# Statistics instructions for the normalisations, and another order of the expert and context products, in a two-layer decoder on one core

## The chip, the cores and the metric

The kernel runs on one core of one Trainium2 chip, as one program. The metric is the device time of one execution in microseconds (us). The kernel before took 1017.04 us as the median of three runs (1016.49 to 1020.86).

## The reference

Input `x` has 4 sequences of 256 tokens with 128 channels, the context 4 x 512 tokens. Six blocks are added to `x` one after the other, each on a layer norm of `x`:

```python
x = x + L0_attn(layernorm(x))          # causal, 16 heads of 8, weights plus low-rank weights
x = x + L0_xattn(ctx, layernorm(x))    # 16 heads of 64; keys: normed context and latents; normed latents ask
x = x + L0_ffn(layernorm(x))           # attention, then 8 routed experts and one shared expert
x = x + L1_attn(layernorm(x))          # causal attention with clipped scores
x = x + L1_xattn(layernorm(x), ctx, ctx, mask)   # one head of 128
x = x + L1_ffn(layernorm(x))           # base product and low-rank experts
# layernorm(x) = (x - mean(x)) / sqrt(var(x) + 1e-5), over the 128 channels
```

`L0_xattn` and `L0_ffn` norm their input, itself a layer norm, once more: `layernorm(layernorm(x))`. `L0_ffn` norms a third time, after its attention and ahead of its experts.

## The kernel before, in words

`x` lies in SBUF as 8 tiles of 128 tokens x 128 channels (`x[P, 8, 128]`). Each engine has its own program, written out by hand in the order in which it runs; semaphores tie them. An engine works strictly in that order, so a wait holds all that is behind it. The stages follow each other: attention `att0`, cross attention, `att1`, experts, `att2`, `single` (the one-head cross attention) and `mixture`. The long loops are inside the attentions (16 groups of four heads) and the cross attention (8 head pairs x 4 sequences x 2). What the change touches are the seams between them.

**Normalisations.** A table `jobs` lists 22 of them, each on four tiles (128 x 512 numbers): `n0` to `n5` (the norm of `x` ahead of each block), `ctx` 0 to 3, and the second norms `lat`, `ln1` (of `z`, written by `again`) and `ln2` (of `xin`). Each job is a chain through three engines. On VectorE `centre` (L1294) adds up each token (L1298) and subtracts the mean (L1299); ScalarE squares the result (`square_jobs`, L1010); VectorE's `variances` adds up the squares (L1306); GpSimd's `rstd_jobs` (L1852) makes the power -1/2 in two instructions (L1857, L1858); VectorE's `scale` multiplies (L1312) and lets the consumer go through `normed`. TensorE then transposes the four tiles (`transposes`, L468), ScalarE copies them out, and products follow (L518 to L521).

**Cross operands.** Between `att0` and the cross attention TensorE multiplies query and key weights (L494) into four banks, ScalarE copies them to `A_all` (L1089), and eight groups of transposes of the context pass through two banks (L508), each copied out by ScalarE (L1100, L1013). ScalarE's program has squares of `n1` ahead of `A_all`, those of `lat` 0 in the middle, those of `lat` 1 ahead of the second four groups. VectorE's `cross_latents` (L1494) comes last before the first query product.

**Shared expert and routing.** SyncE issues the load of the eight experts' first weights (`w1all`) once the cross attention has left its memory, and the shared expert's weights (`w1b`, `w2b`, L435 to L437) when the first half of `xin` is written, into the arena. ScalarE and VectorE split `w1b` into a high and a low part. TensorE runs `shared_up` (three products for each of 8 tiles of hidden numbers), the gate, `shared_down` (64 products), and between these the products that rank and find tokens (`ranks_of`, `tokens_of`). VectorE works the routing out in some 40 small linked instructions; GpSimd then gathers the tokens of 15 sorted tiles by indirect DMA (L1929), and results are scattered back (L1940), fetched (`back`, L447) and added to `x` (L1701).

**Context keys and values.** `single` first makes the keys (`wk4`, four products, L878) and values (`wv4`, 16 products, L883) of the context, which hang on nothing but `ctxT`, written during the cross operands. They lie in the arena, ahead of the queries of the normed `x`.

## Time and profile before

| | us |
|---|---|
| median of the runs | 1017.04 (1016.49 to 1020.86) |
| the profiled execution | 1019.7 |
| its span in the trace | 1017.9 |
| TensorE matmuls busy | 915.8 |
| VectorE busy | 680.0 |
| ScalarE busy | 547.6 |
| GpSimd busy | 205.5 |

The profiled execution lies 2.7 us above the median; its span leaves out 1.8 us of start and end. Busy times are sums over the whole span and say little of the seams. Times in the rows below are us from the start of the span unless marked ns. In a row of the timeline, a bracket gives how long the engine had been idle before the instruction and what released it.

### The profile page before, as it was taken

How to read it: one execution, taken by the hardware profiler on the slowest of the kernel's cores; microseconds unless marked ns; L12 is line 12 of the kernel's file. 1: busy time of each engine (PE TensorE's matmuls, PEld its weight loads, DVE VectorE, ACT ScalarE, POOL GpSimd, SP SyncE). 2: the span in 40 equal slices, each digit the busy share in tenths (PEclk: the TensorE clock that was granted, in tenths of full speed). 3: DMA queues.
4: the chain of work that ended last, by engine and by line, in shares of the span. 5: the costliest groups of instructions: out<-in, count | busy, mean ns of one | idle time of the engine just before them, and what ended most of it. 6: DMA issues, size and time to landing. Idle time of an engine off the chain costs nothing. (4 is left out here: it accounts for less than half of the span.)

```text
span 1017.9 us, 21416 instructions
## 1 busy us (share of the span) xinstructions
PE 915.8 (90%) x6712; PEld 742.9 (73%) x6712; DVE 680.0 (67%) x1706; ACT 547.6 (54%) x1515; POOL 205.5 (20%) x321
## 2 busy tenths in 40 slices
PE   5899968999999999999999699997876788888888
PEld 3677758888888888888888487776766555555665
DVE  5878766666665666666653578885523799999574
ACT  2667655555555555555553267774444466666351
POOL 2544220000000000000000233330153344443100
PEclk9999999999999999999999799999888899999996
DMA  7000000000000000000000200002121000000000
GB/s 267 2 0 0 0 1 1 2 1 1 0 0 0 0 0 0 0 0 0 0 0 1 82 2 0 0 0 81 55 41 51 0 2 0 0 0 0 21 1 21
DMA packets 9398, 16.14 MB, mean 16 GB/s; under 512 B 816, under 2 KB 5040, under 8 KB 8976
## 3 DMA queue, kind: packets, MB, share of 16 engines
q1 hardware_dynamic: 8400, 13.68, 3.9%
q0 software_dynamic: 960, 1.97, 0.9%
q8 instruction: 22, 0.36, 0.1%
q14 instruction: 16, 0.13, 0.0%
HBM read 13.61 MB, written 2.03 MB: 15 GB/s over the span
## 5 line engine op out<-in xcount | busy, mean ns | idle before, releaser
L1514 DVE TENSOR_REDUCE xnegmax<-psum 128x1 f32<-128x768 f32 x128 | 122.3, 955 | 139.8 <-PE psum L649 139.6
L1156 ACT ACTIVATE arena<-psum,xnegmax 128x768 f32<-128x768 f32 x128 | 115.4, 902 | 139.5 <-DVE xnegmax L1514 97.8
L536 PE MATMUL psum<-arena 128*128 (+2 forms) x768 | 187.3, 359 | 1.8 <-POOL arena L1872 0.5
L1872 POOL TENSOR_TENSOR arena<-arena,pack_a 128x256 f32 (+1 forms) x192 | 122.5, 646 | 146.3 <-PE psum L540 71.0
L1051 ACT ACTIVATE arena<-psum,arena 128x256 f32<-128x256 f32 (+1 forms) x256 | 112.1, 445 | 57.7 <-PE psum L555 28.4
L555 PE MATMUL psum<-pack_a,arena 128*128 128x128 f32 x704 | 110.9, 278 | 30.2 <-ACT arena L1058 24.2
L536 PEld LDWEIGHTS psum<-arena 128*128 128x128 f32 x768 | 122.0, 192 | 11.7 <-issue 4.6
L555 PEld LDWEIGHTS psum<-pack_a,arena 128*128 128x128 f32 x704 | 79.8, 142 | 58.6 <-issue 24.3
L667 PE MATMUL psum<-pack_a,arena 128*128 128x128 f32 x768 | 106.8, 275 | 0.2 <-ACT arena L1147 0.2
L647 PE MATMUL psum<-kv_high,xq_high 128*128 128x384 f32 x256 | 101.0, 394 | 3.3 <-DVE xq_low L1503 1.7
L1147 ACT ACTIVATE arena<-psum 128x512 f32<-128x512 f32 x128 | 75.9, 593 | 42.5 <-PE psum L667 42.5
L667 PEld LDWEIGHTS psum<-pack_a,arena 128*128 128x128 f32 x768 | 87.4, 141 | 13.9 <-issue 12.3
L679 PE MATMUL psum<-arena,xv 128*64 128x256 f32 x768 | 89.9, 383 | 0.0
L648 PE MATMUL psum<-kv_low,xq_high 128*128 128x384 f32 x256 | 86.4, 338 | 0.0
L649 PE MATMUL psum<-kv_high,xq_low 128*128 128x384 f32 x256 | 86.4, 337 | 0.0
L1907 POOL COPY acur<-A_all 128x128 f32 (+1 forms) x18 | 5.7, 318 | 387.4 <-PE psum L632 387.4
L1398 DVE COPY arena<-psum 128x384 f32<-128x384 f32 (+1 forms) x96 | 58.9, 616 | 27.0 <-PE psum L555 27.0
L679 PEld LDWEIGHTS psum<-arena,xv 128*64 128x64 f32 x768 | 52.3, 137 | 31.0 <-issue 6.0
L1391 DVE SCALAR_TENSOR_TENSOR arena<-arena,ones_ 128x256 f32<-128x256 f32 x128 | 73.2, 574 | 0.1
L1058 ACT ACTIVATE arena<-psum 128x512 f32<-128x512 f32 (+1 forms) x96 | 55.3, 577 | 3.7 <-PE psum L555 3.6
L540 PE MATMUL psum<-causalb,identb 128*128 128x128 bf16 x256 | 56.3, 220 | 0.0
L639 PEld LDWEIGHTS psum<-pack_v,kvT 128*128 128x128 f32 x396 | 53.9, 191 | 2.7 <-DVE xv L1519 0.9
(282 smaller groups left out, 1670.9 us busy)
## 6 DMA issues: line engine op xcount, KB each, us to landing
w1all<-in_w SPq DMA_DIRECT2D x1, 2048.0 KB, 9.3
arena<-in_w SPq DMA_DIRECT2D x1, 2048.0 KB, 9.4
pack_v<-in_pack_v SPq DMA_DIRECT2D x1, 1088.0 KB, 9.6
pack_l<-in_pack_l SPq DMA_DIRECT2D x1, 1079.5 KB, 12.6
pack_q<-in_pack_q SPq DMA_DIRECT2D x1, 1024.0 KB, 7.4
pack_f<-in_pack_f SPq DMA_DIRECT2D x1, 684.0 KB, 10.7
pack_a<-in_pack_a SPq DMA_DIRECT2D x1, 649.0 KB, 6.4
pack_b<-in_pack_b SPq DMA_DIRECT2D x1, 578.0 KB, 9.5
```

Source lines behind the costliest of these rows:

```text
L536: last = mm(bank[j][:, u * T:u * T + keys], qm[:, j, u * P:(u + 1) * P], kT[:, bass.ds(b * T, keys)], start=True, stop=not a.causal)
L555: last = transpose(bank[4 + j % 2][:, i * P:(i + 1) * P], prob[:, j, u, k * P:(k + 1) * P], ident)
L647: mm(out, xq_high[:, u % 2, tile], kv_high[:, u // 2, keys], start=True, stop=False)
L648: mm(out, xq_high[:, u % 2, tile], kv_low[:, u // 2, keys], start=False, stop=False)
L649: last = mm(out, xq_low[:, u % 2, tile], kv_high[:, u // 2, keys], start=False, stop=True)
L667: last = transpose(bank[4 + (3 * u + c) % 2][:, (2 * i + h) * P:(2 * i + h + 1) * P], xprob[:, u % 2, h * KEYS + kt * P:h * KEYS + (kt + 1 ...
L679: mm(bank[6][XD * a:XD * (a + 1), 0:T], xv[:, b, kt * P + XD * a:kt * P + XD * (a + 1)], xpT[:, b % 2, a, kt * T:(kt + 1) * T], start=(kt ...
L1051: last = activation(prob[:, j, u, 0:keys], bank[j][:, u * T:u * T + keys], ACT.Exp, bias=negmax[:, j, u:u + 1], accum_out=sums[:, it, u * ...
L1147: activation(xpT[:, (mu // 2) % 2, mu % 2, 2 * c * T:2 * (c + 1) * T], bank[4 + (3 * mu + c) % 2][:, :], ACT.Copy).then_inc(sx["pT_act"], 1)
L1156: activation(xprob[:, u % 2, half * KEYS:(half + 1) * KEYS].rearrange("p (c w) -> p c w", c=2), src, ACT.Exp, bias=xnegmax[:, u % 2, half: ...
L1514: v.tensor_reduce(xnegmax[:, u % 2, half:half + 1], banks_pair(half), AX.XY, ALU.max, negate=True)\
L1872: pool.tensor_tensor(qm[:, j, :], qT[:, bass.ds(b * T, T)], headmask[:, bass.ds(g * HG + j, 1)].broadcast_to([P, T]), ALU.mult)\
```

## The change

- **Normalisations.** `centre`, `variances` and the squares on ScalarE are gone, with the memory `centred` and `squares`. `measure` runs four `bn_stats` on 128 x 128 and, after a wait for them, four `bn_aggr`, which write mean and variance. `scale` is four `tensor_scalar` on 128 x 128 (subtract the mean, multiply). The second norms `lat` and `ln1` are not measured: GpSimd works out their factor from the first norm's variance in four instructions. In most places `scale` of the first half now stands behind `measure` of the second.
- **Shared expert.** Its weights get a place of their own (`shared_w`), and their loads are issued right behind `w1all`, without the wait for `xin`. `weight_low` stands ahead of `scale` of the first half. `w1now` moves out of `hid`. `ranks_of` comes ahead of `shared_down`; of `shared_down(1)` one tile comes before `tokens_of`, three after.
- **Context keys and values.** They move from the front of `single` to `context_operands`, behind the experts and ahead of `att2`, in the memory of `w1all`.
- **`mixture`.** TensorE waits for `x_parts` 7 ahead of the gate's bank.

```diff
+        shared_w = sb("shared_w", [P, 2 * B * KEYS - 2 * NT * P - 4 * F])
+        w1b, w2b, iota = shared_w[:, 0:F], shared_w[:, F:F + FT * D], shared_w[:, F + FT * D:F + FT * D + P]
...
-            sp.wait_ge(sf["xin_ready"], 1)
-            sp.dma_start(w1b[:, 0, :], w1_d[E]).then_inc(sf["shared_in"], 16)
+            sp.dma_start(w1b, w1_d[E]).then_inc(sf["shared_in"], 16)
...
                 shared_up(1)
-                shared_down(0, range(0, 2))
                 ranks_of()
-                shared_down(0, range(2, 4))
-                shared_down(1)
+                shared_down(0)
+                shared_down(1, range(0, 1))
                 tokens_of()
+                shared_down(1, range(1, 4))
...
+            def context_operands():
+                pe.wait_ge(sf["gelu_done"], 2 * FT + FT * SORTED)
                 for c in range(4):
+                    if c == 2:
+                        pe.wait_ge(sf["expert_ready"], SORTED)
                     for t in range(4):
                         last = mm(bank[(6, 7, 2, 3)[c]][:, t * P:(t + 1) * P], ctxT[:, (4 * c + t) * P:(4 * c + t + 1) * P],
                                   col("l", "wv4"), start=True, stop=True)
                     last.then_inc(sg["proj_psum"], 1)
+                for c in range(4):
+                    mm(bank[(4, 5, 0, 1)[c]][:, :], col("l", "wk4"), ctxT[:, c * BANK:(c + 1) * BANK], start=True, stop=True)\
+                        .then_inc(sg["proj_psum"], 1)
+                pe.wait_ge(sg["proj_act"], 4)
+                pe.wait_ge(sg["proj_dve"], 4)
...
+            context_operands()
             attention(att2, z, "n3", col("l", "w3"), col("l", "wp3"))
...
+            def measure(keys):
                 for key in keys:
                     k, src, _, (after, value) = jobs[key]
                     dve.wait_ge(after, value)
+                    for t in range(4):
+                        chain.did(v.bn_stats(moments[:, k % 4, t, :], src[:, t, :]))
+                    chain.wait(dve)
+                    for t in range(4):
+                        last = v.bn_aggr(moments_of(key)[:, t, :], moments[:, k % 4, t, :])
+                    last.then_inc(var_ready, 1)
 
             def scale(keys):
...
+                    for t in range(4):
+                        rstd = stat[:, k % 4, 3, t:t + 1]
+                        if key in parents:
+                            last = v.tensor_scalar(dst[:, t, :], src[:, t, :], rstd, None, ALU.mult)
+                        else:
+                            last = v.tensor_scalar(dst[:, t, :], src[:, t, :], moments_of(key)[:, t, 0:1], rstd,
+                                                   ALU.subtract, ALU.mult)
+                    last.then_inc(normed, 1)
...
                 for h in range(2):
...
-                    centre([("ln2", h)])
+                    measure([("ln2", h)])
                     if h:
                         z_low_half(0)
-                    variances([("ln2", h)])
-                    if h == 0:
+                    else:
                         weight_low()
                     scale([("ln2", h)])
...
-                    normalise([("n3", c)])
+                    measure([("n3", c)])
+                scale([("n3", 0), ("n3", 1)])
...
+            measure([("n1", 0)])
             add_to_x(att0.out_psum, 1, 1)
...
+            measure([("n1", 1)])
+            scale([("n1", 0), ("n1", 1), ("lat", 0), ("lat", 1)])
...
+            measure([("n2", 0)])
             add_to_x(sx["out_psum"], 1, 1)
...
+            measure([("n2", 1)])
+            scale([("n2", 0), ("ln1", 0), ("n2", 1)])
...
+                    if key in parents:
+                        parent = jobs[parents[key]][0]
+                        first = stat[:, parent % 4, 3, :]
+                        pool.wait_ge(rstd_ready, parent + 1)
+                        link(pool.tensor_tensor(work, first, first, ALU.mult))
+                        link(pool.tensor_tensor(work, work, moments_of(parents[key])[:, :, 1], ALU.mult))
+                        link(pool.tensor_scalar(work, work, EPS, None, ALU.add))
```

## Rows read from the trace of the kernel before

**Rows 1.** The page, part 1: busy us, share of the span, instructions, by engine.
```profile
PE 915.8 (90%) x6712; PEld 742.9 (73%) x6712; DVE 680.0 (67%) x1706; ACT 547.6 (54%) x1515; POOL 205.5 (20%) x321
```
**Rows 2.** Windows: stretch, length; busy us by engine, PEclk, DMA share, GB/s.
```profile
162.00:570.00 408.00, 405.85 (x2969) 351.08 (x2967) 239.63 (x419) 214.39 (x476) 5.89 (x18) 1.00 0.02 5
...
778.00:790.00 12.00, 1.20 (x9) 0.97 (x8) 3.78 (x9) 1.06 (x3) 2.32 (x4) 0.72 0.20 61
...
802.00:947.00 145.00, 119.29 (x938) 84.61 (x938) 139.28 (x572) 95.92 (x269) 62.27 (x93) 0.99 0.00 0
```
**Rows 3.** Groups: busy, mean ns, idle before and releaser; last, timeline of one scaling.
```profile
L1306 DVE TENSOR_REDUCE stat<-squares 128x4 f32<-128x512 f32 x22 | 14.9, 682 | 7.8 <-ACT squares L1010 7.6
...
L1312 DVE TENSOR_TENSOR z<-centred,stat 128x512 f32<-128x512 f32 x18 | 12.8, 715 | 14.5 <-POOL stat L1858 14.3
...
L1299 DVE SCALAR_TENSOR_TENSOR centred<-stat,x 128x512 f32<-128x512 f32 x12 | 8.3, 692 | 0.4
L1298 DVE TENSOR_REDUCE stat<-x 128x4 f32<-128x512 f32 x12 | 8.2, 684 | 2.9 <-DMA x<-in_x 2.5 <-DVEq L1750 0.2
...
141.20 0.69 DVE L1312 TENSOR_TENSOR z<-centred,stat 128x512 f32<-128x512 f32 x1 [1.41 <-POOL stat L1858]
```
**Rows 4.** VectorE's small instructions: timeline (start, us), and one group.
```profile
24.98 0.29 DVE L1366 TENSOR_REDUCE arena<-psum 128x1 f32<-128x128 f32 x1
...
25.18 0.41 DVE L1369 TENSOR_REDUCE arena<-psum 128x1 f32<-128x256 f32 x1
...
731.18 0.17 DVE L1658 TENSOR_SCALAR chosen<-psum 128x15 uint32<-128x15 f32 x1 [1.38 <-PE psum L808]
731.27 0.16 DVE L1659 SCALAR_TENSOR_TENSOR arena<-psum,pack_f 128x15 f32<-128x15 f32 x1
...
785.41 1.14 DVE L1701 SCALAR_TENSOR_TENSOR x<-arena,x 128x128 f32<-128x128 f32 x4 [5.36 <-DMA arena<-expert_rows]
...
L1673 DVE COPY arena<-w1all 128x512 f32 x15 | 6.4, 427 | 7.7 <-issue 7.7
```
**Rows 5.** Timeline, first groups of att0.
```profile
34.83 0.52 PE L555 MATMUL psum<-pack_a,arena 128*128 128x128 f32 x3 [4.29 <-DVE arena L1398]
```
**Rows 6.** Timeline, cross operands.
```profile
134.31 2.06 PE L494 MATMUL psum<-pack_q 64*128 64x128 f32 x32
...
137.72 1.06 ACT L1089 ACTIVATE A_all<-psum 128x512 f32<-128x512 f32 x2
...
141.65 1.97 PE L508 MATMUL psum<-pack_a,ctx_x 128*128 128x128 f32 x8 [4.26 <-ACT ctxT L1100]
...
148.39 0.81 DVE L1494 TENSOR_SCALAR kvT<-psum,pack_b 128x512 f32<-128x512 f32 x1 [0.75 <-PE psum L468]
```
**Rows 7.** Timeline, from the cross attention to att1.
```profile
572.78 1.09 PE L468 MATMUL psum<-pack_a,z 128*128 128x128 f32 x4 [3.56 <-DVE z L1312]
...
581.12 0.66 PE L468 MATMUL psum<-pack_a,z 128*128 128x128 f32 x4 [1.67 <-DVE z L1312]
```
**Rows 8.** Timeline, from att1 to the first gathered tile.
```profile
706.18 0.66 PE L468 MATMUL psum<-pack_a,z 128*128 128x128 f32 x4 [2.54 <-DVE z L1312]
...
709.19 0.77 PE L778 MATMUL psum<-z_high,w_high 128*128 128x512 f32 x1 [2.35 <-DVE z_low L1582]
...
732.25 1.21 POOL L1929 DMA_INDIRECT arena<-rows,chosen  x1 [21.23 <-DVE chosen L1661]
```
**Rows 9.** The context's products: values as a group, keys in the timeline.
```profile
L883 PE MATMUL psum<-pack_l,ctxT 128*128 128x128 f32 x32 | 4.1, 275 | 0.0
...
958.22 3.60 PE L878 MATMUL psum<-ctxT,pack_l 128*128 128x512 f32 x8
```
**Rows 10.** Timeline, from the experts to att2.
```profile
791.72 1.09 PE L468 MATMUL psum<-pack_a,z 128*128 128x128 f32 x4 [11.99 <-DVE z L1312]
...
800.41 0.75 DVE L1352 TENSOR_SCALAR arena<-psum,pack_l 128x512 f32<-128x512 f32 x1
```
**Rows 11.** Timeline, first scores of single.
```profile
967.02 1.02 PE L896 MATMUL psum<-arena 128*128 128x512 f32 x2
```

More of the change, by code:

```diff
@@ L407, in decoder, with measured, moments_of @@
                     job(("ln2", h), quarter(xin, h), quarter(z2, h), (sf["xin_ready"], h + 1))
+        def measured(key):
+            return sum(1 for other in jobs if other not in parents and jobs[other][0] <= jobs[key][0])
+        def moments_of(key):
+            return stat[:, jobs[key][0] % 4, 0:2, :].rearrange("p a (t s) -> p (a t) s", s=2)
         FIRST_JOBS = [("n0", 0), ("n0", 1)]
@@ L956, in mixture @@
                 pe.wait_ge(sl["zT_act"], 1)
+                pe.wait_ge(x_parts, NT - 1)
                 gate(0)
@@ L1292, in link @@
                 chain.wait(dve)
-            def centre(keys):
+            def measure(keys):
                 for key in keys:
@@ L1696, in experts @@
                     v.tensor_copy(expert_rows[:, i, :], bank[2 + i % 2][:, 0:D]).then_inc(sf["expert_ready"], 1)
+                dve.wait_ge(sf["w1_split"], 1 + SORTED)
+                dve.wait_ge(loaded["l"], 16)
+                for c in range(4):
+                    dve.wait_ge(sg["proj_psum"], c + 1)
+                    v.tensor_tensor(quarter(vx, c), tiles(bank[(6, 7, 2, 3)[c]][:, :]),
+                                    col("l", "bv4").unsqueeze(1).broadcast_to([P, 4, D]), ALU.add)\
+                        .then_inc(sg["proj_dve"], 1)
                 dve.wait_ge(sf["mixed"], 2 + NT)
```

168 lines of the change are left out of this document (47 added, 121 removed).

## The prediction

> **What bounds the kernel now.** I read the page first, then the table of windows by stage, then the groups of instructions, and then the timeline of each seam between two stages. The page gives TensorE 90% of the span [rows 1], but that is a mean over unlike stages. The windows part them: the cross attention keeps TensorE busy for 405.85 of 408 us, the loop of `att2` keeps VectorE busy for 139.28 of 145 us, and behind the experts, from 778 to 790, TensorE has 1.20 us of work in 12 [rows 2]. The diff touches no loop of an attention. What it can win or lose lies in the seams, so I take each seam by itself: what releases TensorE there, and when would that come after the change? VectorE's total busy time matters nowhere.
>
> **Prices.** One measured norm before: sum 0.69, centre 0.69, a wait for ScalarE's square of about 0.75 and the sum of squares 0.69 [rows 3], so some 2.8 us until GpSimd may begin; GpSimd's two steps hold VectorE for 1.41, and the scaling takes 0.69 [rows 3]. After: four `bn_stats`, a wait, four `bn_aggr`. The trace has neither, so I bound them by neighbours. Reductions of 128 columns start 0.20 apart and last 0.29, tiny instructions start 0.09 apart and last 0.17 [rows 4]. Low end: 3 x 0.20 + 0.29 + 0.03, then 3 x 0.09 + 0.17, is 1.36. High end, every instruction at its whole duration: 4 x 0.29 + 4 x 0.17 + 0.03, 1.87. Cheaper than the low end is excluded, since no instruction of either width starts closer; dearer than the high end is not (rivals 3 and 4). I take 1.45, close to the low end, since the four of a row are independent as L1366 and L1369 are. The norm is ready for GpSimd 1.35 us sooner, and VectorE is spared some 0.6 us of work (three instructions of 512 columns against eight small ones). The scaling becomes four instructions of 128 columns: four with one column operand took 1.14 us, 0.26 apart [rows 4]. I take 1.04 for it, 0.35 dearer than now, with 0.8 (0.20 apart) and 1.4 (whole durations of 0.35) as ends. A copy of 512 columns from SBUF to SBUF took 0.427 us [rows 4], faster than the 0.715 of the scaling with two tensors, which speaks for the cheap end.
>
> The Trainium skill ("VectorE: DVE Perf Modes", TRN2 errata) says that each instruction that reads SBUF pays a fixed latency, so that many small tiles pay it many times: a rule that speaks against this change. By its (N+151)/0.96 formula, an estimate, one of 128 columns costs 0.29 us, which is the duration of L1366, while starts 0.20 apart show that much of it overlaps; by that page a measurement would cost at least 1.9 instead of 1.45, the third rival.
>
> **The seams, one by one, in us won.**
> - *Start and first groups of `att0`.* The scaling of `n0` is on the path: -0.35. Between the first two groups VectorE holds TensorE for 4.29 us [rows 5] with context norms. Two centrings and two sums of squares (3.9) become two measurements (2.7), +1.2, and two scalings -0.7. Together +0.2; with the ends of the prices -1.5 to +1.2.
> - *Cross operands.* The first two banks of weight products are full about halfway through L494, at 135.3, but ScalarE copies them out only at 137.72, because squares stand ahead: +2.4. Two more squares in the chain of copies: +1.1. TensorE therefore idles about 1 us instead of 4.26 ahead of the third group of transposes, and eight of them don't take 1.97 [rows 6] but about 1.1 (four took 0.66 at full clock [rows 8]): +0.9. Sum 4.4, some more where waits close up: 4.7. What is late next is the second norm of the latents: two measurements, GpSimd's chain of four steps for each `lat` (two take 1.41 with their waits [rows 3]; four, by an estimate from that, 1.9), the scaling; I get 142.5 for it, and transposes of the context last until 142.3, so both meet. `cross_latents` then starts at 143.6, not 148.39 [rows 6]. 3.7 to 5.3.
> - *Into `att1`.* TensorE has nothing from 569.22 on (572.78 less 3.56 [rows 7]), when the second half of `x` can be added. Now `scale` of `n2` 0 and `ln1` 0 stand behind `measure` of `n2` 1: 0.6 + 1.45 + 1.04 + 0.85 gives 573.2, so the first transposes come 0.4 later. The second half isn't measured any more: its transposes wait 1.67 us today [rows 7]; they would follow the first half's products at once: +1.7. Net +1.3.
> - *`ln2` and the shared weights.* Today the loads start when `xin` is written, and the split of the weights holds `scale`; transposes come 2.54 us after TensorE ran out at 703.64 [rows 8]. Loaded long before, the weights cost VectorE 0.6 inside GpSimd's time. Measured 701.7, factor 703.0, scaled 704.1: +2.0, and `shared_up` moves with it, at 707.1 instead of 709.19. The loads' own issue on SyncE lies behind `w1all`, under the end of the cross attention, and nothing waits there.
> - *Routing.* 16 of the 64 passes of `shared_down` no longer stand ahead of the ranks; they come when VectorE has picked, so about 1.5 sooner. Then 40 passes, then `tokens_of`; the gathers start 2.0 sooner than 732.25 [rows 8] counted from the same start. Three tiles of `shared_down` are now behind them and put the first sorted tile's transpose 0.4 later, but the second is no longer waited for, and the gap there closes. I take +2.0 at the end of the loop; 0 to 3.5.
> - *Context products.* Values 4.1, keys about 3.5 (3.60 with the pass record's tail) [rows 9]: 7.6 us of TensorE in a hole of 11.99 us [rows 10] that ends when `n3` is scaled. They begin at 779.7 and end at 787.4; VectorE's four additions and ScalarE's four copies trail by 0.7, while VectorE would wait for the fetched rows until 785.41 [rows 4]. Cost nothing, with 3.5 us of cover; without cover each us counts.
> - *Into `att2`.* The first half is scaled behind the second's measurement: 785.41 + 1.14 + 1.45 + 1.14 + 1.35 + 1.04 is 791.5, as today. The second half is ready 4.5 us sooner, but TensorE is busy with the first at half clock anyhow. VectorE's memsets come off the path, and query copies no longer begin at 800.41 [rows 10]; the last of those that the scores need ends at 801.0, not 802.4: +1.4.
> - *`single`.* The products ended in scores at 967.02 [rows 11], 8.8 us after they began at 958.22 [rows 9]. After: add 0.7, measure 1.45, scale `n4` 0 1.04 (now behind the second measurement, not under the projection), transposes 0.6, copy 0.65, queries 0.9, VectorE's copy 0.75: 964.5 at full clock, +2.5. TensorE would stand idle 3.2 us first. After 2.54 us it came back at full clock (0.66 for four transposes [rows 8]), after 3.56 at half (1.09 [rows 7]). Half clock would cost two transposes 0.45 each and two passes each of queries and scores 0.86, all but 0.3 of the gain. I take the middle: +1.3.
> - *`mixture`.* `n5` a bit sooner, but TensorE is bound by its base products there: +0.2. The wait for `x_parts` is satisfied by the time of the transposes: 0.
>
> **Sum.** 0.2 + 4.7 + 1.3 + 2.0 + 2.0 + 1.4 + 1.3 + 0.2 = 13.1. The profiled execution of 1019.7 would become 1006.6; the median of the runs lies 2.7 lower, so 1004.
>
> **Rivals.**
> 1. *TensorE stays at full clock in the seams.* Idle times become shorter at three of them. One half's projections are four passes of 512 columns (0.43 each, from the keys) and eight of 128 (0.13) [rows 9], 2.7 us more at half clock. For it: att1's second half, `shared_up`, whose gaps get shorter. Against: the gap ahead of `ln1` 0 grows. Three such places and 1.2 in `single`: 9 us more, 995.
> 2. *The expert loop gives it back.* From the first gather [rows 8] to the hole behind it [rows 2] it takes 46 us for 15 tiles, where GpSimd's gathers and scatters and waits that the trace doesn't explain share the pace. If its end doesn't move, 4.0 are lost: 1008. For it: GpSimd's descriptors are the same; against: they start sooner.
> 3. *The small instructions don't overlap.* Nine measurements at 1.87 (+0.42) and ten scalings at 1.4 (+0.36) on the path cost 7.4: 1011.5. Against: two starts 0.20 apart and two 0.09 apart [rows 4]. The errata rule of "VectorE: DVE Perf Modes" in the Trainium skill speaks for it.
> 4. *Slower.* `bn_stats` or `bn_aggr` is a longer instruction than any that I bound it by. About 115 small ones lie on the path (nine times eight, ten or eleven times four), so the gain is gone at 0.11 us above my price for each; at 0.2 above, 23 us are added and 13.1 won: 1027. Nothing in the trace speaks for it but that neither instruction is in it.
> 5. *The context products don't fit under the wait*, because a bank or the last copy holds them past 791.5: +1 to +4, 1007.
>
> **How the numbers follow.** Forecast 0.50, with its own range of 999 to 1009; rival 1 0.17; rival 2 0.17; rival 3 0.10; rival 4 0.04; rival 5 0.02. The range runs from 992, between rival 1 and the forecast, to 1012, rival 3. A measurement of this kernel can tell about 0.5%, 5 us, from no change. Faster by more than that (under 1012): all but rival 4 and half of rival 3 and a little of the rest, 0.92; within 0.5%: 0.05; slower: 0.03.
>
> **What would show it.** `bn_stats` about 0.20 apart and `bn_aggr` about 0.1; ScalarE's copies to `A_all` right behind the first weight products, and the first cross query some 5 us sooner after `att0`; transposes of `ln2` 0 about 0.5 us behind the projection; 7.6 us of context products inside the hole behind the experts with the clock full, and the hole otherwise as long; scores of `single` 6 us behind its projection. Wrong it would be if TensorE waited longer ahead of the first halves (their scaling is behind a second measurement everywhere), or if the expert loop ended no sooner.

## The result and the profile after

The changed kernel takes 1004.86 us (median of 4 runs, 1003.74 to 1009.54), the kernel before 1017.27 beside it: a ratio of 0.9875 with a 95% interval of 0.9851 to 0.9900, 12.4 us less. A second set of six runs, beside the experiments, gave 1006.95 against 1019.34, 0.9894 (0.9864 to 0.9924). The profiled execution took 1005.44 us, its span is 1003.6 where that of before was 1017.9: 14.3 less, of a forecast of 13.1.

The page's busy times, to be read beside [rows 1], and two windows that answer to [rows 2]: the hole behind the experts (now 767 to 779) and the loop of `att2`.

```profile
PE 916.4 (91%) x6712; PEld 743.2 (74%) x6712; DVE 668.1 (67%) x1850; ACT 534.3 (53%) x1493; POOL 207.7 (21%) x329
...
767.00:779.00 12.00, 7.79 (x47) 5.52 (x46) 8.43 (x33) 2.75 (x4) 3.66 (x6) 0.92 0.19 55
...
790.00:935.00 145.00, 119.53 (x955) 85.36 (x954) 138.97 (x572) 97.61 (x272) 60.75 (x90) 1.00 0.00 0
```

VectorE does 144 instructions more in 11.9 us less, ScalarE has lost 13.3 us of squares, TensorE does the same. In the hole TensorE now works for 7.79 us of 12. The prices of the new instructions, from the groups (busy us, mean ns of one, idle before), to be held against [rows 3]; then one measurement in the timeline:

```profile
L1286 DVE BATCH_NORM_STATS2 moments<-x 128x6 f32<-128x128 f32 x48 | 10.4, 279 | 3.0 <-DMA x<-in_x 2.5 <-DVEq L1733 0.2
...
L1289 DVE BATCH_NORM_AGGREGATE stat<-moments 128x2 f32<-128x6 f32 x72 | 6.8, 157 | 0.6
...
L1303 DVE TENSOR_SCALAR z<-x,stat 128x128 f32<-128x128 f32 x48 | 13.1, 338 | 2.9 <-POOL stat L1834 2.9
L1301 DVE TENSOR_SCALAR z<-z,stat 128x128 f32<-128x128 f32 x16 | 4.7, 353 | 2.1 <-POOL stat L1834 2.0
...
946.08 0.87 DVE L1286 BATCH_NORM_STATS2 moments<-x 128x6 f32<-128x128 f32 x4
946.99 0.38 DVE L1289 BATCH_NORM_AGGREGATE stat<-moments 128x2 f32<-128x6 f32 x4
947.29 1.08 DVE L1303 TENSOR_SCALAR z<-x,stat 128x128 f32<-128x128 f32 x4
```

A measurement takes 1.29 us (946.08 to 947.37) and frees VectorE after 1.21; four scalings take 1.08. The forecast had 1.45 and 1.04.

The seams in the timeline, in the order of [rows 5 to 8], then [rows 10] and [rows 11]:

```profile
33.90 0.87 PE L567 MATMUL psum<-pack_a,arena 128*128 128x128 f32 x3 [3.00 <-DVE arena L1384]
...
135.63 2.06 ACT L1085 ACTIVATE A_all<-psum 128x512 f32<-128x512 f32 x4 [5.47 <-PE psum L506]
...
138.51 1.14 PE L520 MATMUL psum<-pack_a,ctx_x 128*128 128x128 f32 x8 [1.00 <-ACT ctxT L1094]
...
143.75 0.81 DVE L1480 TENSOR_SCALAR kvT<-psum,pack_b 128x512 f32<-128x512 f32 x1 [0.83 <-PE psum L480]
...
568.71 1.01 PE L480 MATMUL psum<-pack_a,z 128*128 128x128 f32 x4 [4.18 <-DVE z L1301]
...
575.79 0.60 PE L480 MATMUL psum<-pack_a,z 128*128 128x128 f32 x4
...
696.64 0.66 PE L480 MATMUL psum<-pack_a,z 128*128 128x128 f32 x4 [1.01 <-DVE z L1303]
...
720.37 1.24 POOL L1904 DMA_INDIRECT arena<-rows,chosen  x1 [19.97 <-DVE chosen L1646]
...
779.44 1.09 PE L480 MATMUL psum<-pack_a,z 128*128 128x128 f32 x4 [4.65 <-DVE z L1303]
...
789.33 0.75 DVE L1338 TENSOR_SCALAR arena<-psum,pack_l 128x512 f32<-128x512 f32 x1 [1.90 <-PE psum L530]
...
948.42 1.11 PE L480 MATMUL psum<-pack_a,z 128*128 128x128 f32 x4 [3.10 <-DVE z L1303]
...
953.14 1.79 PE L914 MATMUL psum<-kvx,arena 128*128 128x512 f32 x2
```

In the brackets stands how long TensorE waited. Ahead of the third group of context transposes it fell from 4.26 us to 1.00, ahead of `ln2` from 2.54 to 1.01, and ahead of the second half of `ln1` from 1.67 to nothing. Ahead of the first halves it grew at two places: 4.18 at `ln1` (3.56 before), and 3.10 at `n4`, where before the change the context's products filled the time. At `n3` it is 4.65 where it was 11.99, but the products of the context (767.62 to 774.79) now fill the rest of that hole. The same instants in both traces, with what the forecast's terms add up to by then:

| begins (us) | before | after | moved | forecast |
|---|---|---|---|---|
| second projection of `att0` | 130.54 | 130.67 | +0.1 | -0.2 |
| first query product, cross attention | 149.30 | 144.66 | -4.6 | -4.9 |
| first scores of `att1` | 587.93 | 579.98 | -8.0 | -6.2 |
| first transposes of `ln2` | 706.18 | 696.64 | -9.5 | -8.2 |
| first gather | 732.25 | 720.37 | -11.9 | -10.2 |
| last expert row copied | 779.76 | 767.82 | -11.9 | -10.2 |
| first scores of `att2` | 802.52 | 790.87 | -11.7 | -11.6 |
| first scores of `single` | 967.02 | 953.14 | -13.9 | -12.9 |
| last addition to `x` | 1014.44 | 1000.18 | -14.3 | -13.1 |

### The profile page after: what moved, and what is told of

It reads as the page before. It is cut to its first block, busy times and chain, and to the rows that moved or that the text cites. A ratio compares the mean times of both kernels' runs of the same rounds, so it can differ in the third digit from the quotient of the medians.

```text
span 1003.6 us, 21535 instructions
## 1 busy us (share of the span) xinstructions
PE 916.4 (91%) x6712; PEld 743.2 (74%) x6712; DVE 668.1 (67%) x1850; ACT 534.3 (53%) x1493; POOL 207.7 (21%) x329
## 4 chain that ended last, share of the span: by engine, by line
PE 75%; DVE 13%; issue 5%; ACT 4%; DMA 1%; DVEq 1%; another core or an unknown queue 0%; ACTq 0%; POOL 0%; SPq 0%
PE psum L548 10%; PE psum L679 9%; PE psum L691 9%; PE psum L567 5%; PE psum L659 5%; PE psum L660 4%; PE psum L661 4%; PE psum L651 4%; DVE arena L1377 4%; PE psum L644 3%; PE psum L585 3%; PE psum L619 2%; DVE arena L1355 2%; PE psum L760 1%; PE psum L591 1%
## 5 line engine op out<-in xcount | busy, mean ns | idle before, releaser
L679 PEld LDWEIGHTS psum<-pack_a,arena 128*128 128x128 f32 x768 | 87.4, 141 | 13.9 <-issue 12.3
```

The lines of the kernel that those rows point to most:

```text
L679: last = transpose(bank[4 + (3 * u + c) % 2][:, (2 * i + h) * P:(2 * i + h + 1) * P], xprob[:, u % 2, h * KEYS + kt * P:h * KEYS + (kt + 1 ...
```

## The experiments

Ratios are to the kernel before, run beside each group; an interval is 0.0020 to 0.0038 to either side. Since the program's beginning and end differ from one profile to the next (below), stretches inside the traces are compared, not instants.

### What each part is worth

The third part undone (`e1_context_back`; abridged. On VectorE the scaling of the first half of `n4` also goes back under the projection, as before the change, so the two are measured together):

```diff
-            context_operands()
             attention(att2, z, "n3", ...)
 def single():
+    for c in range(4): mm(bank[2 + c], wk4, ctxT[c]) ...
+    values(0); values(1); transposes n4 0; values(2); queries(0); values(3); transposes n4 1
```

> The changed kernel with the third part alone undone: keys and values of the context are multiplied inside single again, in the old order (keys, two values, transposes, the rest), and nothing stands in the hole behind the experts. The recorded theory: behind the experts they cost nothing, and in single they were mostly beside the normalisation already, so that the move is worth about 1.3 us there: this kernel takes 0.8 to 1.8 us more than the changed one, all of it between the last projection of att2 and the first scores of single. A rival: the products and the four additions on VectorE delay n3 (the changed kernel's transposes of n3 come 5.9 us after the rows are fetched, 779.44 less 773.49, against 6.3 before, 791.72 less 785.41); then the first transposes of n3 come sooner after the fetched rows here than 5.9 us, and the kernel is within 0.5 us of the changed one. A second rival: 7.2 us of TensorE work (3.74 and 3.60) stood on the path of single, and 4 us or more come back.

1006.19 us, 0.9885 (0.9860 to 0.9910), beside 0.9875 and 0.9894 for the changed kernel: level with it. The transposes of `n3` come 5.95 us behind the fetched rows (774.73 to 780.68), as in the changed kernel (5.95), so the products delay nothing there. The first scores of `single` come 8.6 us behind the last projection of `att2` (945.36 to 953.99), 7.8 in the changed kernel: the move wins 0.8 us there, the low end of what the theory gave (1.3 in e2 and e6 below, whose `single` is that of the changed kernel, at a granted clock of 0.68 over the four us from 948, where it was 0.50 in the changed kernel's profile), and the 7.2 us of products were nearly all hidden in the old place too. That is too little to be seen in times that scatter by 6.

The second part undone (`e2_shared_back`), its order alone undone (`e6_order_back`), and the changed kernel itself beside the latter (`e0_changed`):

```diff
+            sp.wait_ge(sf["xin_ready"], 1)          # e2 only
             sp.dma_start(w1b, w1_d[E])...
+                shared_down(0, range(0, 2))         # e2 and e6
                 ranks_of()
-                shared_down(0)
-                shared_down(1, range(0, 1))
+                shared_down(0, range(2, 4))
+                shared_down(1)
                 tokens_of()
-                shared_down(1, range(1, 4))
```

> The changed kernel with the second part undone: the loads of the shared expert's weights wait for xin again, and two tiles of shared_down stand ahead of the ranks again, all others behind them and ahead of tokens_of. The recorded theory: the weights' loads cost 1.5 to 2.0 us ahead of the first transposes of ln2 (in the changed kernel these follow the projection after 1.01 us; here again after some 2.5), and the order of the products 2.0 to 2.5 us, seen at the first gather and again at the end of the loop over the sorted tiles: 3.5 to 4.5 us more than the changed kernel. The rival that the loop over the sorted tiles gives it back, paced by the gathers and scatters and by stalls that do not move: the first gather comes 3.5 to 4.5 us later but the last expert row only 1.5 to 2.0 later, and so does the kernel.

> The changed kernel with the old order of the products alone: two tiles of shared_down ahead of the ranks, the others behind them and ahead of tokens_of; the weights are loaded as in the changed kernel. The recorded forecast gives the order 2.0 us at the end of the loop: 2 us more than the changed kernel beside it. Theory A: the first gather comes 0.7 to 2 us later against the end of the picks, but the loop from the first gather to the last expert row takes 47.5 instead of 50: equal to the changed kernel or up to 1.5 us less. The transposes of ln2 come about 1 us behind the projection as in the changed kernel, not 2.7 as with the loads undone.

> The changed kernel itself once more, beside the three below on the same chip: its median there, and a second profile of the same program. Two stretches are looked at. The loop over the sorted tiles, from the first gather to the last expert row, took 47.45 us in its profile (720.37 to 767.82), but 50.14, 49.91 and 50.67 in the three experiments that have the same order of shared_down, and 47.51 and 47.65 in the two kernels with the old order (the kernel before, and the changed kernel with the second part undone). Theory A: the new order brings the gathers 2 us forward and the loop gives it back, so that 47.45 was an exception: here 49 to 51. Theory B: the loop varies by 3 us in any order; then nothing is foretold. The other stretch is mixture, from the last addition in single to the last addition to x: 24.29 us there, 23.1 to 29.0 in the others. Theory: the same instructions, at TensorE's half clock for a shorter or longer part; 22.5 to 29 here, the more the longer the granted clock is at half.

e2: 1004.30 us, 0.9855 (0.9835 to 0.9876). e6: 1004.20, 0.9856 (0.9832 to 0.9880). e0: 1006.95, 0.9894 (0.9864 to 0.9924). e2 was expected 3.5 to 4.5 us slower than the changed kernel, and is not slower. The new order of the products wins nothing; by the medians of e6 and e0 it costs 2.7 us, but their intervals overlap, and at the last expert row the traces differ by 1.1 us (620.9 and 622.0 behind the first cross scores). The traces say why nothing is won. Start of the first gather, the restart of the loop and the first expert row, in e0 (new order) and in e6 (old order):

```profile
717.72 1.24 POOL L1904 DMA_INDIRECT arena<-rows,chosen  x1 [19.93 <-DVE chosen L1646]
...
724.04 2.08 PE L838 MATMUL psum<-arena 128*128 128x128 f32 x8 [0.39 <-issue]
...
726.13 1.91 PE L838 MATMUL psum<-arena 128*128 128x128 f32 x8
...
729.35 0.43 DVE L1658 COPY arena<-w1all 128x512 f32 x1 [2.96 <-PE psum L838]
729.36 1.14 ACT L1193 ACTIVATE arena<-psum,pack_f 128x128 f32<-128x128 f32 x4 [5.01 <-PE psum L838]
...
730.64 0.58 PE L848 MATMUL psum<-arena 128*128 x1 [2.60 <-ACT arena L1193]
...
732.75 0.29 DVE L1681 COPY arena<-psum 128x128 f32<-128x128 f32 x1 [2.97 <-PE psum L848]
```

```profile
720.26 1.24 POOL L1904 DMA_INDIRECT arena<-rows,chosen  x1 [22.20 <-DVE chosen L1646]
...
727.26 1.14 ACT L1193 ACTIVATE arena<-psum,pack_f 128x128 f32<-128x128 f32 x4 [1.35 <-issue]
...
730.41 1.06 PE L838 MATMUL psum<-arena 128*128 128x128 f32 x8
...
731.88 0.29 DVE L1681 COPY arena<-psum 128x128 f32<-128x128 f32 x1 [4.21 <-PE psum L848]
731.89 1.14 ACT L1193 ACTIVATE arena<-psum,pack_f 128x128 f32<-128x128 f32 x4 [3.14 <-PE psum L838]
```

In e0 the first tile's products begin at 724.04 and take 2.08 us by the record (a matmul's end is modelled), but ScalarE's gelu of them begins only at 729.36, 3.2 us behind that end; in e6 it begins 0.14 us behind it. VectorE and ScalarE stand still and go on together, 11.64 us behind the first gather. The brackets say for what: both wait for TensorE's signal that these products are done. TensorE itself does not stand with them: its records show the second tile's products from 726.13 to 728.04, then it waits 2.60 us for ScalarE's gelu and goes on at 730.64. The expectation of e9 below counts it among the engines that go on together, which is not what these rows show. In e6 VectorE and ScalarE go on 11.62 us behind the first gather, again at signals of TensorE (which by its records still works at 730.41), but there the first gelu (727.26) and the first tile's second product came ahead of the standstill. The gather is 2.3 us earlier in e0 counted from the first cross scores, the first tile is not, and the standstill catches it one stage less far. So the loop, from the first gather to the last expert row, takes:

| order | profiles | us |
|---|---|---|
| old | before, e2, e6, e5, e11 | 47.5, 47.7, 47.7, 47.7, 47.6 |
| new | after; e0, e1, e3, e4, e7, e8, e10 | 47.4; 51.1, 50.1, 49.9, 50.7, 51.0, 51.0, 50.1 |

The profile of the changed kernel was the exception (there they went on at +10.12 us); seven others of the same order took 2.5 to 3.7 longer, e3 among them, where they went on at +10.91.

The loads' place was worth 2.3 us where the forecast put it (the first product of the shared expert is 550.3 us behind the first cross scores in e6 and 552.5 in e2), and nothing at the gather (573.2 us behind them in e6, 573.0 in e2): with early weights and the old order the picks are ready at 710.43 and the ranks' product starts at 712.23, behind two tiles of `shared_down`; with late weights it starts 0.25 behind the picks. Late weights with the new order were not run.

The normalisations alone (`e5_norms_alone`: both diffs above on the changed kernel):

> The changed kernel with the second and the third part undone together: the normalisations by statistics instructions alone (with the squares gone from ScalarE). The recorded forecast sums the parts so: 13.1 in all, of which the order in the routing 2.0, the shared weights some 1.0 to 2.0, the products of the context and what hangs on them about 1: the normalisations alone some 8 to 9, 4 to 5 us more than the changed kernel. What the experiments say so far: the context products back cost nothing measurable, the order back won about 2.7 us, the loads back cost 1.7 at their place, so this one is level with the changed kernel or up to 2 us faster: 1004 to 1007, and nearly all of the gain of 13 us is that of the normalisations.

1010.16 us, 0.9911 (0.9888 to 0.9934): 8.6 us less than before by the medians, the 8 to 9 of the forecast's sum rather than my expectation. Its profile is of a run of 1002.82, and the six other runs took 1008.75 to 1011.40, so what makes most of its runs slower than e2's (1003.37 to 1006.27), which differs by the context products' place alone, is in no trace here; all that is on record of them is the granted clock over the whole run, 0.961 to 0.967 in those six and 0.967 to 0.970 in e2's. With the new order there was no such difference (e1 against e0). Whether the move behind the experts is worth 0 or some 5 us stays open.

### What paces the loop over the sorted tiles

Four gathers ahead (`e9_four_gathers`), twelve ahead (`e10_twelve_gathers`):

```diff
-AHEAD = NT        # 8
+AHEAD = 4         # e9; 12 in e10
```

> The changed kernel with four gathers issued ahead instead of eight; the others follow behind the scatters, one each, as before. In eight of the ten profiles so far TensorE, VectorE and ScalarE stand still in the loop over the sorted tiles and go on together 11.61 to 11.68 us after the first gather began, when the eight gathers (1.25 us apart, the last ends 10.0 us after the first began) and their transfers are done; with the new order of shared_down this stands ahead of the first tile's gelu, with the old order behind it, and the loop from the first gather to the last expert row takes 50.0 to 51.1 instead of 47.5 to 47.7. Theory: the standstill belongs to the row of gathers and ends when its transfers are done. With four it ends some 6.6 us after the first gather, before the first gelu is due (8.4 us), so the first expert row comes some 3 us sooner (12 us behind the first gather, not 15), the loop takes 46 to 48 us and the kernel 2 to 4 us less than the changed kernel, if GpSimd, which now alternates scatter and gather (2.57 us a pair) for eleven tiles instead of seven, does not set the pace. Rival: the standstill has to do with the code of the loop (its first pass through it) and not with the gathers: it stays at the same place, and the kernel is not faster.

> The changed kernel with twelve gathers issued ahead instead of eight. Theory (the standstill belongs to the row of gathers): the engines go on together some 16.6 us after the first gather began, not 11.65, or stand still twice; the first expert row comes 18 to 20 us behind the first gather, not 15; behind it the loop is faster, since GpSimd has only three gathers left among the scatters. Rival (it belongs to the code of the loop): they go on at 11.65 as before and the loop is the same or shorter.

e9: 1018.57 us (twelve runs, 1016.21 to 1026.40, the profiled one 1025.74), 1.0004 (0.9980 to 1.0028), as slow as before the change. e10: 1005.67 over six runs, of which one took 1811.43 us, for a cause that no trace shows; the other five took 1002.05 to 1012.22, median 1004.52, ratio 0.9865 (0.9827 to 0.9902), level with the changed kernel. First e9, then e10:

```profile
719.05 1.24 POOL L1904 DMA_INDIRECT arena<-rows,chosen  x1 [19.95 <-DVE chosen L1646]
...
731.09 0.29 DVE L1681 COPY arena<-psum 128x128 f32<-128x128 f32 x1 [3.11 <-PE psum L848]
...
734.77 1.00 POOL L1915 DMA_INDIRECT expert_rows<-arena,chosen  x1 [0.30 <-issue]
736.07 0.97 POOL L1904 DMA_INDIRECT arena<-rows,chosen  x1 [0.30 <-issue]
737.02 0.33 PE L830 MATMUL psum<-pack_a,arena 128*128 128x128 f32 x1 [3.99 <-DMA arena<-rows,chosen]
```

```profile
718.72 1.24 POOL L1904 DMA_INDIRECT arena<-rows,chosen  x1 [19.94 <-DVE chosen L1646]
...
736.09 0.29 DVE L1681 COPY arena<-psum 128x128 f32<-128x128 f32 x1 [6.71 <-remote]
736.09 1.14 ACT L1193 ACTIVATE arena<-psum,pack_f 128x128 f32<-128x128 f32 x4 [5.37 <-remote]
```

Both halves of the theory hold for the standstill: with four gathers the common restart at +11.6 is gone and the first expert row comes at +12.04 as expected; with twelve VectorE and ScalarE go on at +17.37 (16.6 expected), after a shorter halt of both that ends at +10.23, and the first row is copied at +17.37. It goes with the number of gathers in a row, not with the code. That the shorter row makes the kernel faster was wrong: behind it TensorE waits for each gather (3.99 us at 737.02), which now follows a scatter, and the loop takes 63.7 us. With twelve it takes 50.1, of which the part behind the first row takes 32.7, where it took 36.1 in e0. In e10's brackets stands "remote", a releaser that the profile could not name; by the program VectorE waits there for TensorE's second product and ScalarE for its first one, as in e6. Why TensorE's signals come so late while gathers are issued the traces don't say.

### The first half scaled ahead, and TensorE's clock

`e3_first_ahead`:

```diff
             measure([("n2", 0)])
+            scale([("n2", 0), ("ln1", 0)])
             add_to_x(sx["out_psum"], 1, 1)
             measure([("n2", 1)])
-            scale([("n2", 0), ("ln1", 0), ("n2", 1)])
+            scale([("n2", 1)])
```

and so for `n3` and `n4`, where the copy of the first queries and the first scores also come ahead of the second scaling and the second transposes.

> The changed kernel, but with the first half scaled before the second half is measured: in front of att1 (n2 and ln1 of the first half scaled before the second half is added to x), in front of att2 (n3) and in single (n4, where the copy of the first queries is ahead of the second scaling too, and the first scores ahead of the second transposes). Theory: the forecast's step that named the scaling behind a second measurement was right on the place and too small on the price, because VectorE waits 5.6 us for the second half of the projection (564.57) when it could scale: TensorE's wait of 4.18 us ahead of ln1 goes nearly to zero, the wait ahead of n3 loses 1.1, and the scores of single come 3 to 4.5 us sooner, TensorE's clock with them. 7 to 10 us less than the changed kernel, some 996. Rival: the second half, whose measurement and scaling nothing brings forward, is what is late next; the gain is then 2 us at att1, 0 at att2 and 2 in single: 3 to 5 us, some 1001.

1003.77 us (999.45 to 1004.55), 0.9836 (0.9813 to 0.9858), against 0.9875 and 0.9894 for the changed kernel: 4.0 and 5.9 us less by the ratios (1.1 and 3.2 by the medians), near the rival's 3 to 5 and far from the theory's 7 to 10. The first of the two pairs of intervals overlaps a little. Ahead of `att1`:

```profile
561.73 0.60 PE L480 MATMUL psum<-pack_a,z 128*128 128x128 f32 x4
...
567.63 2.00 DVE L1300 TENSOR_SCALAR z<-z,stat 128x128 f32<-128x128 f32 x4
567.79 2.33 POOL L1849 TENSOR_TENSOR arena<-arena,pack_a 128x256 f32<-128x256 f32 x4 [0.33 <-DVE arena L1337]
...
569.68 1.11 PE L480 MATMUL psum<-pack_a,z 128*128 128x128 f32 x4 [3.55 <-DVE z L1300]
```

TensorE's wait ahead of the first half is gone (4.18 us in the changed kernel), and 3.55 of it stand ahead of the second, with half clock behind it. From the first cross scores to the first scores of `att1` it is 429.8 us against 430.7. Ahead of `att2`, from the fetched rows to the first scores, 15.95 against 17.38 and 16.90 (changed kernel, e0), but e1, e2, e5 and e6, without this edit, have 16.0 to 16.2: only the first transposes are surely sooner, 5.42 behind the fetched rows instead of 5.95. In `single` it works in full: the first scores come 3.3 us behind the first transposes of `n4` instead of 4.7, and those 0.7 behind the projection instead of 3.1.

Eight products that nothing reads ahead of `n3` (`e4_filled`):

```diff
+                pe.wait_ge(sg["proj_dve"], 2)
+                for _ in range(8):
+                    mm(bank[7][:, :], col("l", "wk4"), ctxT[:, 0:BANK], start=True, stop=True)
```

> The changed kernel with eight more products of 512 columns (128x512, 0.43 us each at full clock, 3.4 us) on TensorE behind the context products, into a bank whose contents are done with; nothing reads them. They fill most of the 4.65 us in which TensorE stands still ahead of the transposes of n3 and release nobody. Theory: the half clock there (four transposes 1.09, two key and query products 2.07 and 1.91, eight value products 1.92 us) comes from the standstill: filled, they take 0.6, 1.1, 1.0 and 1.05, and the first scores of att2 come 2.5 to 3.3 us sooner, the kernel 2 to 3.3 us less. Rival: the clock falls behind the experts for another reason (the load of the loop before), and the products change nothing or delay the transposes by up to 0.5: 0 to 0.5 us more.

1007.90 us (1002.18 to 1011.82), 0.9886 (0.9855 to 0.9918).

```profile
775.84 7.03 PE L902 MATMUL psum<-ctxT,pack_l 128*128 128x512 f32 x16
...
782.71 0.60 PE L480 MATMUL psum<-pack_a,z 128*128 128x128 f32 x4
```

I had sized them wrongly: 0.43 us is one of the two passes of such a product, so eight take 7.03 and put the transposes 2 us late. But the clock is the theory's: four transposes in 0.60, at full clock, where they took 1.09 behind a standstill of 4.65 us, and the first scores follow them by 8.0 us, where the nine profiles with the old wait have 10.0 to 11.5. As the transposes are 2 us late, the kernel is no faster.

Products at the end (`e7_end_filled`), and the first half ahead with three products at `n3` and those at the end (`e8_ahead_filled`):

```diff
+                    if n >= NT - 1:                 # single's loop, behind the weighted sums
+                        mm(bank[6][:, :], col("l", "wk4"), ctxT[:, 0:BANK], start=True, stop=True)
                 transposes("n5", z, 0, sl["zT_psum"])
+                mm(bank[7][:, 0:T], col("l", "wk4"), ctxT[:, 0:T], start=True, stop=True)
```

(the last line behind the second transposes of `n5` too)

> The changed kernel with products that nothing reads in TensorE's standstills near the end: one of 512 columns (0.88 us) in each of the last three steps of single's loop, and one of 256 columns (0.44 us) behind each of the two groups of transposes of n5, where TensorE waits 0.7 to 0.8 us for the copy. Theory: the granted clock falls to half some 5 to 8 us after the sparse stretch at the end of single and stays there for 8 to 25 us, by chance; without the sparse stretch it stays at full, and mixture, from the last addition in single to the last addition to x, takes 22 to 23 us in place of 23 to 29: median 1.5 to 3 us less than the changed kernel beside it, and the spread of the runs smaller. Rival: the fall comes for another reason (the many small products, or the ones with 6 columns and with one row), mixture is no shorter, and the products add up to 0.5 us.

> The first half scaled ahead of the second half's measurement everywhere (as in the third experiment), three products of 512 columns that nothing reads behind the context products (2.64 us, so that they end before n3 is scaled; the eight of the fourth experiment lasted 7.03 and put the transposes 2 us late), and the products of the experiment before at the end. Theory: the three gains add up: 2.4 us at att1, 0.5 and 2.5 to 3 at att2 (four transposes 0.6, key and query products at 1.1 and 1.0, first scores under 10.5 us behind the fetched rows, not 16 to 17), 5 at single, 2 in mixture: 993 to 997, and every part of it seen at its place in the profile. Rival: VectorE, which holds att2's loop and single's for most of the time, or the second halves take most of it: 999 to 1002.

e7: 1009.61 us, 0.9904 (0.9872 to 0.9936), slower than e0 by 2.7 us in the medians, but the intervals overlap almost wholly. `mixture` took 24.11 us in its profile and 24.26 in e0's. The clock fell all the same, in the middle of the one-row and 128-column products of `base` (2.00 us windows of e7, the granted clock is the third figure from the end):

```profile
982.00:984.00 2.00, 2.00 (x15) 1.64 (x14) 0.82 (x4) 0.00 (x0) 1.06 (x2) 1.00 0.00 0
984.00:986.00 2.00, 2.00 (x9) 1.42 (x8) 0.29 (x2) 0.00 (x0) 0.00 (x0) 0.73 0.00 0
986.00:988.00 2.00, 2.00 (x8) 1.66 (x8) 0.01 (x1) 0.00 (x0) 0.00 (x0) 0.50 0.00 0
```

That stretch is dense, and in the 10 us before it TensorE's longest wait is 0.54 us: no long standstill stands ahead of this fall, and the rival holds. e8: 1001.42, 0.9821 (0.9797 to 0.9846), between theory and rival. At `n3` the theory fails: the transposes ran at full clock (0.63 us for four) behind a wait of 1.62, but the queries and keys behind them at half (1.74 and 1.91), and the first scores came 15.1 us behind the fetched rows, not under 10.5. In `mixture` it kept full clock for longer (mean 0.79 over 23.8 us). `mixture` differs most between the profiles. The whole of `mixture`, from the last addition in `single` to the last addition to `x`, in e5, e0, e3 and e4, same columns:

```profile
974.45:997.57 23.12, 21.30 (x88) 14.03 (x85) 11.48 (x43) 3.10 (x6) 1.27 (x2) 0.74 0.00 1
```
```profile
976.39:1000.65 24.26, 22.75 (x88) 14.56 (x85) 11.47 (x44) 3.21 (x6) 1.27 (x2) 0.69 0.00 1
```
```profile
970.75:998.72 27.97, 26.46 (x87) 16.87 (x85) 11.47 (x43) 3.21 (x6) 1.26 (x2) 0.58 0.00 1
```
```profile
974.92:1003.94 29.02, 27.51 (x88) 17.54 (x85) 11.49 (x44) 3.21 (x6) 1.26 (x2) 0.55 0.00 1
```

The same instructions take 23.1 us at a mean granted clock of 0.74 and 29.0 at 0.55: 5.9 us that no edit of `mixture` made (e9 took 29.2). The runs of one kernel scatter by about as much, but with one profile of each it isn't shown that this is where.

What pays, together (`e11_best`: e3, the old order, three products ahead of `n3`):

> What the experiments point to, put together: the changed kernel with the first half scaled ahead of the second half's measurement (third experiment), the old order of shared_down (two tiles ahead of the ranks, the others ahead of tokens_of), three products of 512 columns that nothing reads in the standstill ahead of n3, and none at the end. Theory: the gains add up, since they lie at different places: against the changed kernel's 1005 to 1007, 2.5 us less at att1, 1 to 2.5 in the routing and the loop (the loop from the first gather to the last expert row 47.7 instead of 51, the first gather 1.9 later behind the picks), 2 at att2, 4 in single; 997 to 1000, and below both kernels in every run. Rival: the stretch behind the experts takes them back, through TensorE's clock in mixture: 1001 to 1003, as in the eighth experiment.

1002.52 us (998.38 to 1003.28) beside 1021.44 for the kernel before, 0.9816 (0.9786 to 0.9845): the lowest ratio of all, though e8's 0.9821 can't be told from it, and every run is below each run of the kernel before beside it by 13 us or more. The theory's 997 to 1000 is missed. The parts are at their places: from the first cross scores to the last expert row 617.8 us, against 622.0 in e0; from the fetched rows to the first scores of `att2` 14.0 against 16.9, at full clock throughout; from the projection to the scores of `single` 4.0 against 7.8. But the loop of `att2`, from its first scores to its last projection, took 156.1 us, where it took 154.5 in the changed kernel and in ten of the other experiments (156.1 in e9, 155.9 before the change): of the 2.9 us won ahead of it, 1.6 are given back. Counted from the first cross scores it is 8.3 us ahead of e0 at the last addition in `single`, and 4.9 at the last of all: `mixture` took 27.70 us, at a clock of 0.58. That is the rival's case.

## Why the prediction was right, step by step

The time was forecast at 1004 and is 1004.86, and the traces differ by 14.3 us where 13.1 were summed. It lies well inside the range, but partly by luck: the sum holds since errors of both signs met, and the second set of runs gave 1006.95.

- *Prices.* The scaling was right (1.08 for 1.04). The measurement was mis-sized, 1.29 for 1.45, and lies below the low end of 1.36. `bn_aggr` starts 0.07 us apart, closer than the 0.09 of [rows 4]; "no instruction starts closer" was said of the neighbours, and excluded nothing. The rule of small instructions (the Trainium skill, "VectorE: DVE Perf Modes", TRN2 errata) gives about the duration of one (0.29 by its formula, 0.28 measured), not the pace of four (0.20 apart). That ends rivals 3 and 4. By that formula, an estimate, a measurement comes to 1.85, not "at least 1.9". In `att0` two measurements are put at 2.7 where 1.45 each is 2.9, and the two centrings and sums of squares at 3.9 where the rows give 4.1, which leaves the difference of 1.2.
- *Start and `att0`.* +0.2 was forecast, -0.1 came. The wait in the middle shrank from 4.29 to 3.00 as reckoned, but in the twelve experiments the first query product, always 14.0 us behind the second projection, begins anywhere from 142.0 to 144.6 (144.66 here), so a term of 0.2 meant nothing. (The start itself varies so between profiles of the same program: 144.66 and, in e0, 142.18.)
- *Cross operands.* 4.7 forecast, 4.8 measured from the second projection, by the steps named: copies at 135.63, third transposes 1.00 behind, `cross_latents` at 143.75 for 143.6. This is the largest term, and no run puts the squares alone back on ScalarE: it is read from the traces, and e5 bears it out only together with the other normalisations.
- *Into `att1`.* First transposes forecast 0.4 later, measured 0.6. The second half has no wait any more, as forecast, and also runs at full clock: two passes of queries in 1.13 us instead of 2.07. That is rival 1 at one place, and makes 3.3 us of 1.3.
- *`ln2`.* 2.0 forecast, 1.6 measured; GpSimd's first step takes 0.57 us there, 0.25 elsewhere. `shared_up` is at half clock as before.
- *Routing.* The step that failed. The gathers do come 2.3 sooner, and the profile shows 2.4 at the loop's end, but seven other profiles show that the loop gives it back (rival 2, put at 0.17): VectorE and ScalarE get TensorE's signal only when the row of gathers is through, and the new order is caught a stage earlier. That the +2.0 came out in this profile is luck. The forecast took the first gather for the pace; the first tile's products, behind three more tiles of `shared_down`, and that late signal set it. Why the signal is late stays open.
- *Context products.* In the hole, 7.2 us for 7.6, and nothing waits for them: as forecast, and rival 5 is gone.
- *Into `att2`.* +1.4 forecast, -0.3 measured (17.1 us from the fetched rows to the first scores before, 17.4 after, but 16.9 in e0 and 16.0 to 16.2 in e1, e2, e5 and e6: +0.2 to +1.1). The memsets did leave the path, but the value products ran at half clock (1.92 us instead of 1.05 for eight), so TensorE's order set the second half. I had named that clock ("busy with the first at half clock anyhow") and not priced its length.
- *`single`.* +1.3 forecast, +0.8 measured, at half clock as feared (the terms of the forecast's sum give 964.3, not 964.5). "Full clock behind 2.54 us" was read from the transposes of `ln2` alone: `shared_up` behind them ran at half clock before the change too. Another 1.4 us were won in the loop of `att2`, which the forecast left alone and which I can't explain (155.9 to 154.5; e9 and e11 have 156.1).
- *`mixture`.* +0.2 forecast, +0.4 from the first scores of `single` on; but its own length goes with the clock, 23.1 to 29.2 us.

What would make it wrong was named: TensorE waiting longer ahead of the first halves. It does, and e3 shows what that costs the kernel, some 4 to 6 us by the ratios.

## What to carry to other kernels

A reduction of 128 columns by statistics instructions and a scaling by two column operands paid here where three passes over 512 columns and a trip to another engine stood, even on the path. When a half is scaled first, ask what the engine does between: VectorE waited 5.6 us for the second half (until 564.57), the last 4.2 of them with the factor of the first ready. And an order that starts a transfer sooner was worth nothing here, since what came next was not ready sooner: look for the signal that several engines wait for.

## What the runs showed of the hardware

- Four scalings of 128x128 by one column took 0.88 us at 140.07 in the changed kernel, with none of GpSimd's 128x256 products beside them, and 2.00 us beside four of these (2.33, each 0.61 as in most other places), at 567.63 in e3 and in the changed kernel's `ln1` too. The Trainium skill ("SBUF — State Buffer", Who interferes with whom) says that a VectorE instruction of this kind can hold ports that GpSimd needs, and blocks or is blocked; the trace agrees.
- With indirect gathers in a row VectorE and ScalarE stand still together, both waiting for TensorE's signals: until 11.6 us behind the first of eight in eight of the first ten profiles (10.12 and 10.91 in the other two), 17.4 with twelve, with no common restart with four. The Trainium skill ("SBUF — State Buffer", Who interferes with whom) says that a DMA never contends with a compute engine; it speaks there of the ports to SBUF, and no run here shows whether the late signals have to do with those.
- The granted clock was 0.5 (1.2 of 2.4 GHz) behind TensorE's waits of 3.10, 4.18 and 4.65 us (`n4`, `ln1`, `n3`) in the changed kernel's profile, on average 0.68 behind the same 3.10 in e2's (948 to 952), and 1.0 behind the one of 1.00 ahead of the context's third transposes. It also fell from 1.0 to 0.5 within a dense run of products with one row or few columns (e7, 984 to 986). With products that nothing reads in the standstill ahead of `n3` it was 1.0 behind it in e4 and e11; in e8, with the same three products as e11 and a wait of 1.62 us left (1.45 in e11), it was 1.0 for the transposes and fell to 0.5 while the queries ran.
